# Moving the router, a transpose bank and the routing chain inside one software-pipelined attention step

## The reference, cut to what matters

```
x = x + tanh(g_xattn[1]) * L1_xattn(layernorm(x), ctx, mask)     # 16 heads, 77 keys each
x = x + tanh(g_ffn[1])   * L1_ffn(layernorm(x))                  # 32 experts, 4 chosen, room for 256 rows each

# L1_xattn: softmax(Q K^T / 8) V W_O, for each head
# L1_ffn:
logits = x @ gate_w.T;  probs = softmax(logits);  topk_w, topk_idx = top_k(probs, 4)
slot   = position of the token in its expert's queue (running count over all tokens), cut at 256
buf[expert, slot] = x;  out = sum of expert(buf) * weight + shared expert
```

## Time and profile before

| what | value |
|---|---|
| median of three executions | 1023.62 us (1015.46 to 1024.27) |
| the profiled execution | 1024.65 us, span 1022.6 us |
| PE, DVE, POOL, ACT busy | 86%, 62%, 55%, 49% of the span |
| mean granted TensorE clock | 0.926 of full speed |
| the attention loop of layer 1 | from about 508 to 837 us of the span |
| one step in its steady part | 9.58 us |

### The profile page before, as it was taken

How to read it: one execution, slowest core, us unless ns; L and a number is a source line. 1 busy time by engine, 2 the same in 40 slices (tenths; PEclk the granted TensorE clock), 3 DMA queues, 4 the chain that set the end, 5 groups by cost and what they waited for, 6 DMA issues and landing times. The chain is left out here.

```text
span 1022.6 us, 18469 instructions
## 1 busy us (share of the span) xinstructions
PE 879.8 (86%) x5433; PEld 744.1 (73%) x5433; DVE 632.6 (62%) x2000; ACT 501.4 (49%) x1813; POOL 564.0 (55%) x635
## 2 busy tenths in 40 slices
PE   4998777999999979889199899999999978999940
PEld 3564446888888779889188889899898857888720
DVE  4603114688778857557278889999999843444441
ACT  1321654444544246546086778878878822222200
POOL 1400113466666727557448777767777653877851
PEclk8987997899999989999699999999999979999975
DMA  9630788367987888996499924514444205899687
GB/s 305 218 100 0 226 240 203 92 204 223 277 260 221 283 260 276 316 332 225 150 165 257 226 94 180 178 58 140 121 153 140 64 12 149 155 224 250 73 211 159
DMA packets 157812, 189.70 MB, mean 186 GB/s; under 512 B 16035, under 2 KB 137017, under 8 KB 157714
## 3 DMA queue, kind: packets, MB, share of 16 engines
q1 hardware_dynamic: 109810, 121.87, 39.9%
q0 software_dynamic: 30720, 46.46, 20.8%
q10 hardware_dynamic: 17184, 20.19, 5.8%
HBM read 96.19 MB, written 103.63 MB: 195 GB/s over the span
## 5 line engine op out<-in xcount | busy, mean ns | idle before, releaser
L1938 ACT ACTIVATE att<-bank,mx 128x77 f32<-128x77 f32 x512 | 159.0, 343 | 1.0 <-DVE mx L2019 0.9
L1879 POOL DMA_INDIRECT slots_d<-rows,place x128 | 131.4, 1027 | 36.4 <-issue 35.5
L1938 ACT ACTIVATION_READ_ACCUMULATOR att<-bank,mx 128x1 f32 x512 | 115.6, 226 | 0.0
L999 POOL DMA_INDIRECT y_d<-rows x78 | 77.3, 991 | 62.3 <-DVE rows L1377 34.7
L959 POOL DMA_INDIRECT slots_d<-rows,place x64 | 65.2, 1019 | 19.0 <-issue 19.0
L1399 PE MATMUL bank<-wd_hi,act_hi 128*128 128x256 f32 (+1 forms) x206 | 66.5, 323 | 1.3 <-DVE act_lo L1372 0.7
L1893 POOL DMA_INDIRECT acc_d<-expert_out,target_rows x32 | 49.6, 1550 | 26.8 <-issue 23.1
L953 POOL TENSOR_TENSOR act_lo<-prod,act_hi 128x512 fp32r<-128x512 f32 x28 | 36.8, 1313 | 39.9 <-ACT act_hi L1035 39.8
L2019 DVE TENSOR_REDUCE mx<-bank 128x6 f32<-128x462 f32 (+1 forms) x96 | 55.1, 573 | 5.6 <-PE bank L2193 4.9
L1401 PE MATMUL bank<-wd_hi,act_lo 128*128 128x256 f32 (+1 forms) x206 | 58.4, 284 | 0.0
L1400 PE MATMUL bank<-wd_lo,act_hi 128*128 128x256 f32 (+1 forms) x206 | 58.3, 283 | 0.0
(11 more groups left out here) (318 smaller groups left out, 3009.9 us busy)
## 6 DMA issues: line engine op xcount, KB each, us to landing
rows<-slots_d SPq DMA_DIRECT2D x39, 260.0 KB, 4.3
slots_d<-zrow SPq DMA_DIRECT2D x8, 1168.0 KB, 10.8
expert_rows<-slots_d SPq DMA_DIRECT2D x32, 292.0 KB, 3.7
expert_gate_up<-in_wgu SPq DMA_DIRECT2D x28, 256.0 KB, 4.1
x_res<-y_d POOLq DMA_DIRECT2D x14, 512.0 KB
wqk_d<-wqk SPq DMA_DIRECT2D x32, 154.0 KB, 3.5
vwo_d<-vwo SPq DMA_DIRECT2D x16, 308.0 KB
x_res<-in_x SPq DMA_DIRECT2D x8, 512.0 KB, 8.5
```

Source lines behind the costliest of these rows:

```text
L999: pool.indirect_dma_start(y0_d, bass.IndirectOffsetOnAxis(ap=x_rows(s)[:, b, D:D + 1].bitcast(I32), axis=0), y_rows(s, b), None, bounds_ch ...
L1879: pool.indirect_dma_start(slots_d, bass.IndirectOffsetOnAxis(ap=place[:, n % 3, k:k + 1], axis=0), rows[:, n % 3, :], None, bounds_check=S ...
L1938: last = act.activation(att[:, par, h * S:(h + 1) * S], bank[:, a, i * S:(i + 1) * S], ACT.Exp, scale=-1.0, bias=mx[:, par, h:h + 1], accu ...
```

## The change

Four things are edited, all in the loop's `step` functions:

1. PE: the router's matmuls leave their place ahead of `values_mm` and go behind its first three chunks. The transposes of tile r's rows write bank 3 instead of bank 5; for that they wait for `at_out` (the first group's half has been read) instead of `av_added`, and ACT's copy to xbT waits also for `at_T` 3n, that is until PE has finished the third group of attention transposes into the same bank.
2. PE: the two position matmuls of tile m go from the step's start to behind the first scores and transposes.
3. DVE: the layer-norm sums of tile n-2 and the largest score of group 0 go ahead of the slot numbers; `norm_b` goes between the first instruction on slot numbers and the second (the one that sets `pos_read`).
4. DVE: the division of the first 12 heads goes ahead of the routing chain.

ACT's order is as before, with the added wait.

```diff
@@ ACT step
                         if routes:
                             act.wait_ge(b_T, n - 1)
-                            act.activation(xbT[:, :, (n - 2) * P:(n - 1) * P], bank[:, 5, D:2 * D].rearrange("p (k t) -> p k t", k=KD),
+                            if values:
+                                act.wait_ge(at_T, 3 * n)
+                            act.activation(xbT[:, :, (n - 2) * P:(n - 1) * P], bank[:, 3, D:2 * D].rearrange("p (k t) -> p k t", k=KD),
                                            ACT.Copy).then_inc(b_xT, 1)
@@ DVE step
+                        if added:
+                            dve.wait_ge(av_added, n - 1)
+                            sums("b", n - 2, par)
+                            stats("b", n - 2, par)
+                        if scores:
+                            largest(n, par, 0)
                         if dispatch:
                             dve.wait_ge(pos_mm, m + 1)
                             pos = bank[:, 6, 0:E1]
                             picked = chain.mark(dve.tensor_tensor(far[:, mp, :], pos, full[:], ALU.is_ge))
-                        if added:
-                            dve.wait_ge(av_added, n - 1)
-                            sums("b", n - 2, par)
+                        if routes:
+                            norm_b(r, par)
                         if dispatch:
                             chain.need(picked)
                             dve.scalar_tensor_tensor(slot[:, mp, :], far[:, mp, :], FAR, pos, ALU.mult, ALU.add)\
                                .then_inc(pos_read, 1)
-                        if added:
-                            stats("b", n - 2, par)
-                        if dispatch:
                             dve.wait_ge(pos_read, m + 1)
                             want(dve, sent[m % 3], 16 * K1 * (m // 3))
                             dve.max(place[:, m % 3, :], slot[:, mp, :]).then_inc(place_ready, 1)
-                        if scores:
-                            largest(n, par, 0)
-                        if routes:
-                            norm_b(r, par)
...
                         if ahead:
                             low_a(n + 1, 1 - par)
+                        if scores:
+                            inv = inverse(n, par, 0, HP, 2)
+                            chain.need(inv)
+                            scale_heads(par, 0, HP).then_inc(att_ready, 1)
                         if routes:
                             dve.wait_ge(r_mm, r + 1)
                             dve.max(t8[:, par, :], logits1).then_inc(top_ready, 1)
...
-                        if scores:
-                            inv = inverse(n, par, 0, HP, 2)
-                            chain.need(inv)
-                            scale_heads(par, 0, HP).then_inc(att_ready, 1)
@@ PE
+                    ROUTER_AT = 3
+
+                    def router(r):
+                        pe.wait_ge(b_xT, r + 1)
+                        want(pe, ew_ready, r)
...
+                        last.then_inc(r_mm, 1)
+
-                    def values_mm(n, par):
-                        pe.wait_ge(vwo_in, 64 * (n // 8 + 1))
-                        want(pe, av_added, n)
-                        for j in range(JC):
+                    def values_mm(n, first, end):
+                        if first == 0:
+                            pe.wait_ge(vwo_in, 64 * (n // 8 + 1))
+                            want(pe, av_added, n)
+                        for j in range(first, end):
...
                     def step(n, par, scores, values, routes, dispatch):
                         m, mp, r = n - 3, 1 - par, n - 2
-                        if dispatch:
-                            pe.wait_ge(msel_ready, m + 1)
-                            pe.wait_ge(a_xT, min(n + 1, TILES))
-                            to = bank[:, 6, 0:E1]
-                            pe.matmul(to, tri[:], mselb[:, mp, :], start=True, stop=False)
-                            pe.matmul(to, allone[:], cum[:, mp, :], start=False, stop=True).then_inc(pos_mm, 1)
                         for a in range(3):
+                            if a == 1 and dispatch:
...
                             if a == 2 and scores and n + 1 < TILES:
                                 want(pe, pos_read, m + 1)
                                 transpose_a(n + 1, 1 - par)
...
                         if routes:
                             pe.wait_ge(b_xn, r + 1)
-                            pe.wait_ge(av_added, r + 1)
+                            pe.wait_ge(at_out, 3 * min(n - 1, TILES - 1) + (1 if values else 3))
                             for k in range(KD):
-                                last = pe.transpose(bank[:, 5, D + k * P:D + (k + 1) * P], rows[:, r % 3, k * P:(k + 1) * P], ident[:])
+                                last = pe.transpose(bank[:, 3, D + k * P:D + (k + 1) * P], rows[:, r % 3, k * P:(k + 1) * P], ident[:])
                             last.then_inc(b_T, 1)
                         if values:
                             transpose_att(n - 1, 1 - par, 2)
+                        if values:
+                            values_mm(n - 1, 0, ROUTER_AT)
                         if routes:
...
+                            router(r)
                         if values:
-                            values_mm(n - 1, 1 - par)
+                            values_mm(n - 1, ROUTER_AT, JC)
```

More of the change, by code:

```diff
@@ L2232, in transpose_att @@
                         last.then_inc(at_T, 1)
-                    def values_mm(n, par):
-                        pe.wait_ge(vwo_in, 64 * (n // 8 + 1))
-                        want(pe, av_added, n)
-                        for j in range(JC):
+                    ROUTER_AT = 3
+                    def router(r):
+                        pe.wait_ge(b_xT, r + 1)
+                        want(pe, ew_ready, r)
+                        if r == 0:
+                            pe.wait_ge(w3_in, 48)
+                        for k in range(KD):
+                            last = pe.matmul(bank[:, 7, 256:256 + E1], xbT[:, k, r * P:(r + 1) * P], wr1[:, k, :],
+                                             start=k == 0, stop=k == KD - 1)
+                        last.then_inc(r_mm, 1)
[4 more added lines that the diff above has]
+                        for j in range(first, end):
                             if j % 4 == 0:
@@ L2243, in values_mm @@
                                             hi, lo, j == 0, j == JC - 1)
-                        last.then_inc(av_mm, 1)
+                        if end == JC:
+                            last.then_inc(av_mm, 1)
                     def step(n, par, scores, values, routes, dispatch):
                         m, mp, r = n - 3, 1 - par, n - 2
-                        if dispatch:
-                            pe.wait_ge(msel_ready, m + 1)
-                            pe.wait_ge(a_xT, min(n + 1, TILES))
-                            to = bank[:, 6, 0:E1]
-                            pe.matmul(to, tri[:], mselb[:, mp, :], start=True, stop=False)
-                            pe.matmul(to, allone[:], cum[:, mp, :], start=False, stop=True).then_inc(pos_mm, 1)
-                        for a in range(3):
+                        for a in range(3):
+                            if a == 1 and dispatch:
+                                pe.wait_ge(msel_ready, m + 1)
+                                pe.wait_ge(a_xT, min(n + 1, TILES))
+                                to = bank[:, 6, 0:E1]
+                                pe.matmul(to, tri[:], mselb[:, mp, :], start=True, stop=False)
+                                pe.matmul(to, allone[:], cum[:, mp, :], start=False, stop=True).then_inc(pos_mm, 1)
                             if a == 2 and scores and n + 1 < TILES:
@@ L2269, in step @@
                             transpose_att(n - 1, 1 - par, 2)
+                        if values:
+                            values_mm(n - 1, 0, ROUTER_AT)
                         if routes:
-                            pe.wait_ge(b_xT, r + 1)
-                            want(pe, ew_ready, r)
-                            if r == 0:
-                                pe.wait_ge(w3_in, 48)
-                            for k in range(KD):
-                                last = pe.matmul(bank[:, 7, 256:256 + E1], xbT[:, k, r * P:(r + 1) * P], wr1[:, k, :],
-                                                 start=k == 0, stop=k == KD - 1)
-                            last.then_inc(r_mm, 1)
+                            router(r)
                         if values:
-                            values_mm(n - 1, 1 - par)
+                            values_mm(n - 1, ROUTER_AT, JC)
                     steps_pipelined(first, step)
```

## The result

The change makes the kernel slower: 1082.97 us median (1080.64 to 1085.57, four executions) against 1023.21 (1015.46 to 1024.27, four), a ratio of 1.0609 with a 95% interval of 1.0564 to 1.0655 (the quotient of the two medians is 1.0584). The profiled execution took 1083.73 us with a span of 1081.7. The forecast was 1073, in a range from 1056 to 1088.

The account below looks back on a forecast made before the run. Bound: a loop through DVE, ACT and PE, 11.44 us a step. 28 x 11.44 plus 11.05 give 331.4, +48.0 over 283.33; with +1.3 behind it, 1024.65 becomes 1074.0, or 1073 against the median. Range 1056 to 1088.

Parts of the forecast that it names:

- The decisive step: DVE and ACT: `ngm` waits for largest logits behind the 1.30 division, so group 2's exponentials run after it; sum 3.02.
- the predicted step: DVE loop if group 2 isn't held, routing chain still between the divisions: 10.66 a step; as a rival, 1050, chance 0.06.
- The loop of 11.44: New loop through DVE, ACT and PE, from one first-heads reciprocal to the next: 11.44 us a step.
- the 1.70 through PE: From `transpose_a` on PE through the third attention transposes to ACT's xbT copy: 1.70 us.
- Both branches: Ways to ACT's xbT copy: by the largest score, 8.22 (11.05 a step alone), and by `pos_read`, 8.61 (11.44).
- The old loop of 9.42: Loop of DVE and ACT in the kernel before: 9.42 us, 0.16 below its step of 9.58.
- The stall of 0.42: PE's wait at the router in the kernel before, released by ACT's xbT copy: 0.42 us a step.
- PE's 9.16: What PE needs for a step without its stall at the router: 9.16 us.
- The sum: Whole kernel: +48.0 us over 29 loop steps and +1.3 behind the last reciprocal, together +49.3.
- The clock falls: Rival on PE: granted clock drops to 1.2 GHz in the longer steps; 12.7 a step, 1109 us, chance 0.05.
- last sign of being wrong: PE in the loop: the prediction is wrong if PEclk there is well below 1.
- The early steps: First loop steps, held to about 11 us by POOL's extra DMAs: gain or lose little; 5 us more if surplus stays.

Follow-up runs that it names:

- x6: The kernel before with only the first heads' division moved ahead of DVE's routing chain; 1059.6 us, ratio 1.0391.
- x4: The changed kernel with `ngm` (negated largest logit) moved on ACT behind the exponentials of group 2; 1044.9 us, ratio 1.0273.
- x2: The changed kernel with `norm_b` put back behind both slot instructions on DVE; 1059.2 us, ratio 1.0393.
- x7: The kernel before with only the router behind three value chunks, its transposes in bank 3 and both waits; 1013.89 us, ratio 0.9960.
- x9: x8 with the router's matmuls ahead of all ten value chunks again; 1030.98 us, ratio 1.0133.
- x8: The changed kernel with routing chain ahead of the division, `norm_b` behind slot instructions, and routing weights moved behind the largest score of group 0; 1013.2 us, ratio 0.9953.
- x5: The changed kernel with 14 useless matmuls on PE ahead of its wait for `pos_read`; 1073.01 us, ratio 1.0521.
- x1: The changed kernel with DVE's routing chain put back ahead of the first heads' division; 1025.76 us, ratio 1.0066.

## Why the prediction was right, point by point

- *The decisive step, first heads ahead of the routing chain, holds.* ACT waits at `ngm` in every step (1.57), the four exponentials of group 2 run after the division, and x6 has 1.50 of the 1.90 us a step from this edit alone. x4 takes away only the hold and gets the predicted step to 0.02. The Trainium skill ("PSUM — Partial Sum Buffer", "Engine vs sequencer instructions") states that ScalarE's queue is strictly first in, first out. The trace agrees: ACT stood idle at all 29 waits at `ngm`, although the exponentials of group 2 behind it had their largest scores, in the step shown since 662.03, 4.8 us before `ngm` started.
- *The loop of 11.44 measured 11.48.* The sums on DVE agree to 0.08 at each place, being a little long, and the 1.70 through PE was 0.12 short, so the total is better than its terms. Both branches were right too: 11.05 by the largest score (x2: 11.05), and `pos_read` as the later one.
- *The old loop of 9.42*, only 0.16 below the step, was the reason to expect little from the router. x7 shows 9.40. The stall of 0.42 was real (x9 has one back), but it was not worth 0.42. Below that loop the prediction has PE's 9.16 next. x8 shows a branch of 9.35 ahead of it, through the low half and bank 3, a wait that the prediction named (`at_out`) and put at nothing. In the changed kernel, with steps of 11.48, it costs nothing.
- *The sum.* Predicted +49.3, measured +59.1 of span. Of the 9.8 that are missing, the steps at full clock account for 1.4 (28 x 11.48 and 11.35 make 332.8, predicted 331.4), the head of the loop for 0.9 and the tail for 0.1. The other 7.4 are the excess of 340.19 over 332.8; x5, at full clock, takes 6.6 us less for the same steps, the last of which has 11.07 there.
- *The step that was mis-sized* is the rival "The clock falls". I gave it a chance of 0.05 as all or nothing, at 12.7 a step, by one row of 11 us whose PE was busy 9.58 at full clock. That window belongs to the kernel before, whose longest gap of PE in the loop is 1.28. The fall came in 13 of 29 steps, 12 of which took 11.7 to 12.4, and cost 6.6 us in all, where the sum had nothing and the rival 36. By its last sign of being wrong, a PEclk in the loop well below 1, the prediction is partly hit: it is 0.94.
- *The early steps* gave up nearly all their surplus, as the sum had it: from step 2 to step 9 they took 11.48 to 12.36 instead of 9.6 to 11.2, and 11.50 to 11.66 at full clock (x5).
- *Some luck in the range.* The forecast's own bounds for a step gave 1072 to 1082; 1083 lies within 1088 only by the 5 us kept for early steps that didn't give up their surplus. They did, and the clock used that room.

## What to carry to other kernels

Before moving an instruction behind a long one, look who on another engine waits for it and what stands behind that waiter: here a copy of one number held four exponentials, and a division that had covered them came to lie in series. Sum the loop through two engines' lists around one step as well as each engine's own work; a stall of the busiest engine is worth only the distance to the next longest loop. And each reordering that frees one loop should be read against the lists of all engines, POOL's too, since a later signal there came back as a wait in the same loop.

## What the runs showed of the hardware that was not expected

The granted clock of TensorE fell to 0.50, which is 1.2 GHz, behind an idle stretch of 2.24 us in a loop whose PE was otherwise busy, and it stayed at 1.00 behind stretches of 1.48 (the next step), 1.6 (x2) and 1.4 (x4, 17.1 us in 12 steps). It didn't fall every time: of the 17 gaps of 2.21 to 2.34 us in that loop 13 were followed by a fall, and one of 2.34 in x5 (ahead of 861.54) and one of 2.04 in x2 (ahead of 849.52) were not. Two single falls came behind shorter gaps, of 1.96 in x4 (at 555 us) and of 1.88 in x1 (at 570 us); one of 1.97 in x4 (at 544 us) had none behind it. What tells these cases apart stays open. Each slow step makes the next gap of the changed kernel shorter (0.85 to 1.52), and no fall followed one of those, so the dips come at most in every second step. Filling the gap with matmuls whose result is thrown away kept the clock at 1.00 and took 6.6 us, 0.6%, off the loop.
